# Layer 0 of a fused four-layer kernel: its setup and its units become one program, which also makes the start of layer 1

## Time and profile before

| what | value |
|---|---|
| median of 3 runs | 1658.1 us (1653.25 to 1659.24) |
| the profiled execution, its own time | 1658.67 us |
| its span, first to last instruction | 1656.9 us |
| mean granted TensorE clock | 0.971 |
| PE busy | 1541.7 us (93%) |
| DVE busy | 1102.9 us (67%) |
| ACT busy | 673.1 us (41%) |
| POOL busy | 451.4 us (27%) |

### The profile page before, as it was taken

The page is one execution under the profiler, slowest core; times in us unless marked ns, Lnnn a source line. Parts: engine busy times, 40 slices in busy tenths (PEclk is TensorE's granted clock), DMA queues, the critical chain, the costliest instruction groups (busy, mean ns, idle before and its releaser), DMA issues. The chain is left out here.

```text
span 1656.9 us, 33073 instructions
## 1 busy us (share of the span) xinstructions
PE 1541.7 (93%) x13299; PEld 1321.7 (80%) x13299; DVE 1102.9 (67%) x2371; ACT 673.1 (41%) x1270; POOL 451.4 (27%) x532
## 2 busy tenths in 40 slices
PE   4987999999999999999999999879988859999799
PEld 2666888888888888888888888869867747888598
DVE  6886666666666676666666667555599945676444
ACT  4654434343333434433343434432366633544322
POOL 2004120020101211210200200232188866653211
PEclk9998999999999999999999999889989979999899
DMA  4000010010000000000100100020030000000000
GB/s 132 1 0 26 14 39 14 1 39 14 27 14 14 27 14 14 27 14 14 39 14 1 39 27 1 30 45 1 2 115 2 1 1 2 2 2 3 1 26 25
DMA packets 44580, 34.16 MB, mean 21 GB/s; under 512 B 10770, under 2 KB 41496, under 8 KB 44312
## 3 DMA queue, kind: packets, MB, share of 16 engines
q1 hardware_dynamic: 44440, 32.17, 6.7%
HBM read 30.00 MB, written 2.10 MB: 19 GB/s over the span
## 5 line engine op out<-in xcount | busy, mean ns | idle before, releaser
L946 DVE STREAM_TRANSPOSE att_pt<-att_prob 32x256 f32<-32x256 f32 x496 | 215.9, 435 | 6.4
L846 ACT ACTIVATE g_q_sb<-psum,g_cols 128x512 f32<-128x512 f32 x128 | 88.4, 690 | 321.0 <-PE psum L714 321.0
L763 PE MATMUL psum<-g_wo_hi,att_ot_hi 128*128 128x256 f32 x512 | 150.2, 293 | 2.5 <-DVE att_ot_lo L959 1.4
L917 DVE TENSOR_REDUCE att_rmax<-psum 128x6 f32<-128x390 f32 (+1 forms) x96 | 49.2, 512 | 151.3 <-PE psum L676 151.3
L763 PE MATMUL psum<-g_wo_lo,att_ot_hi 128*128 128x256 f32 x512 | 145.5, 284 | 0.0
L763 PE MATMUL psum<-g_wo_hi,att_ot_lo 128*128 128x256 f32 x512 | 145.4, 284 | 0.0
L746 PE MATMUL psum<-att_pt,att_v_sb 128*128 128x128 f32 x1024 | 128.9, 280 | 3.5 <-DVE att_ot_lo L959 3.5
L969 DVE TENSOR_TENSOR g_x_res<-psum,g_x_res 128x256 f32<-128x256 f32 x128 | 54.3, 424 | 116.8 <-PE psum L763 88.5
L746 PEld LDWEIGHTS psum<-att_pt,att_v_sb 128*128 128x128 f32 x1024 | 123.2, 194 | 7.8 <-DVE att_ot_lo L959 3.7
L849 ACT ACTIVATE att_k_sb<-psum,g_cols 128x512 f32<-128x512 f32 x128 | 88.2, 689 | 81.0 <-PE psum L714 81.0
L714 PE MATMUL psum<-split_feat_hi,g_wide_hi 128*128 128x512 f32 x256 | 103.7, 405 | 4.5 <-DVE split_feat_lo L993 3.3
(11 more groups left out here) (301 smaller groups left out, 3936.5 us busy)
## 6 DMA issues: line engine op xcount, KB each, us to landing
g_ctx_f<-in_L_xattn_wq SPq DMA_DIRECT2D x32, 128.0 KB, 2.3
g_ctx_f<-in_L_xattn_wk SPq DMA_DIRECT2D x32, 128.0 KB, 2.8
g_ctx_f<-in_L_xattn_wv SPq DMA_DIRECT2D x8, 512.0 KB, 3.8
g_ctx_f<-in_L_xattn_wo SPq DMA_DIRECT2D x8, 512.0 KB, 3.8
c_ctx_tok<-in_ctx SPq DMA_DIRECT2D x4, 512.0 KB, 5.5
g_x_res<-in_x SPq DMA_DIRECT2D x4, 512.0 KB, 8.7
g_w<-in_L_xattn_mlp_w SPq DMA_DIRECT2D x2, 1024.0 KB
out<-g_x_res SPq DMA_DIRECT2D x8, 256.0 KB, 2.2
```

The source lines that it names most:

```text
L763: mm = pe.matmul(o_ps[p % 2], a, b, start=(h == 0 and t == 0), stop=(not last and h == HG - 1 and t == 2))
L846: act.activation(q_sb[:, h, :], q_ps[:, :], ACT.Identity, bias=G.cols[:, layer, head:head + 1]).then_inc(q_ready, 1)
L917: dve.tensor_reduce(rmax[:, a:b], s_ps[group][:, :, :], X_AXIS, ALU.max).then_inc(max_done, 1)
L946: turned = dve.transpose(pt[to:to + 32, :, :, r, u, 32 * a:32 * a + 32].rearrange("p h a t -> p (h a) t"), by_pair[of:of + 32, :, u, 32 * ...
```

## The change

`phase_setup` and `phase_layer0` become `phase_first`, one program, with its 18 steps (16 units, two of drain) written out and no loop. In it:

- The folding of `Wl` and `Wo` no longer waits for the constant rows; their transposes come on PE after unit 4, their copies on DVE after unit 5.
- ACT normalises 6 context tiles ahead of the units, and 5 each in units 0 and 1. DVE still normalises all 16 tiles of `x` ahead of unit 0, but each is announced by itself.
- POOL's copies of the context are gone: PE reads the context tile itself.
- SP issues layer 1's first weights right behind the constant rows.
- Work of layer 1's prologue moves in: DVE aggregates blocks 0 and 1 after units 8 and 11, POOL inverts; DVE normalises block 0 after units 10 and 12 (two tiles each); PE transposes it after units 13 and 14; ACT makes `raw` after the exponentials of 13 and 14, and the high parts after those of 14 and 15; DVE makes `feat_lo` in steps 16 and 17, behind the output of units 14 and 15; ACT and POOL split the weights of heads 0 and 1 in step 16.
- Layer 1's loop starts at j = 0. POOL's first work there, after a memset, is heads 2 and 3; DVE's is to normalise block 1, and then `wv_hi`, `wv_lo` and two memsets.

The core of the diff:

```diff
-                mm.then_inc(cols_psum, 1)
+                    if u == 4:
+                        pe.wait_ge(rows_in, n_rows)
+                        for i in range(2):
+                            mm = pe.transpose(cols_ps[:, i, :], rows[:, i, :], G.ident[0:ROWS, 0:ROWS])
+                        mm.then_inc(cols_psum, 1)
+                    if u in (13, 14):
+                        features(u - 13)
...
+                def features(k):
+                    pe.wait_ge(G.normed_done, PPB)
+                    pe.wait_ge(G.raw_done, k) if k else pe.wait_ge(cols_kept, 1)
+                    for i in range(PPB):
+                        mm = pe.transpose(x_bank[:, i * P:(i + 1) * P], w.normed[:, i, k * P:(k + 1) * P], G.ident[:, :])
+                    mm.then_inc(G.feat_psum, 1)
...
+                def normalize_context(p):
+                    act.activation(G.xn[:, PAIRS + p, :], G.ctx_tok[:, p, :], ACT.Identity,
+                                   bias=shift[:, p:p + 1], scale=rstd[0][:, p:p + 1]).then_inc(ctx_normed, 1)
+
+                def raw_features(k):
+                    act.wait_ge(G.feat_psum, k + 1)
+                    act.activation(w.raw[:, k, :], x_bank[:, :], ACT.Identity, bias=G.cols[:, 0, 82 + k:83 + k],
+                                   scale=G.cols[:, 0, 80 + k:81 + k]).then_inc(G.raw_done, 1)
+
+                def high_features(k):
+                    act.wait_ge(G.raw_done, k + 1)
+                    act.activation(G.feat_hi[:, k, 0:BLK], w.raw[:, k, :], ACT.Copy).then_inc(G.hi_done, 1)
...
+                    for p in range(EARLY + 5 * u, EARLY + 5 * u + 5):
+                        if p < PAIRS:
+                            normalize_context(p)
...
+                    if u in (13, 14):
+                        raw_features(u - 13)
+                    if u in (14, 15):
+                        high_features(u - 14)
+                    if u == PAIRS:
+                        act.wait_ge(arrived, 16 * len(w.first_loads))
+                        for h in range(2):
+                            act.activation(w.wqk_hi[:, h, :, :, :], w.stage_qk[:, h, :, :, :], ACT.Copy).then_inc(w_high, 1)
...
+                    if u in (8, 11):
+                        blk = (u - 8) // 3
+                        dve.wait_ge(G.stats_kept, PPB * (blk + 1))
+                        for p in range(PPB):
+                            dve.bn_aggr(G.mv[:, blk, p, :], G.stats[:, PPB * blk + p, :]).then_inc(G.mv_done, 1)
+                    if u in (10, 12):
+                        dve.wait_ge(G.rstd_done, 1)
+                        for p in (0, 1) if u == 10 else (2, 3):
+                            dve.tensor_scalar(w.normed[:, p, :], G.x_res[:, p, :], G.mv[:, 0, p, 0:1], G.rstd[:, 0, p:p + 1],
+                                              ALU.subtract, ALU.mult).then_inc(G.normed_done, 1)
+                    if u >= PAIRS:
+                        k = u - PAIRS
+                        dve.wait_ge(G.hi_done, k + 1)
+                        dve.tensor_tensor(G.feat_lo[:, k, 0:BLK], w.raw[:, k, :], G.feat_hi[:, k, 0:BLK].bitcast(F32),
+                                          ALU.subtract).then_inc(G.feat_ready, 1)
...
-                for j in range(-1, NI + 3):
+                for j in range(NI + 3):
```

More of the change, by code:

```diff
@@ L190, in _ @@
                         pool.tensor_tensor(rstd[t][:, ps], rstd[t][:, ps], G.minus_half[:, 0:PAIRS // 2], ALU.pow).then_inc(rstd_done[t], 1)
+                for blk in range(2):
+                    pool.wait_ge(G.mv_done, PPB * (blk + 1))
+                    r = G.rstd[:, blk, :]
+                    pool.tensor_scalar(r, G.mv[:, blk, :, 1], 1e-5, None, ALU.add).then_inc(G.eps_added, 1)
+                    pool.wait_ge(G.eps_added, blk + 1)
+                    pool.tensor_tensor(r, r, G.minus_half[:, 0:PPB], ALU.pow).then_inc(G.rstd_done, 1)
@@ new lines, in scores @@
+                def scores(u):
+                    pe.wait_ge(mix_done, u + 1)
+                    if u:
+                        pe.wait_ge(exp_done, 4 * u)
+                    for b in range(2):
+                        for th in range(2):
+                            mm = pe.matmul(s_ps[b][:, th, :], mix[64 * b:64 * b + 64, 0, th * P:th * P + P],
+                                           mix[64 * b:64 * b + 64, 1, :], start=True, stop=True)
+                        mm.then_inc(s_psum, 1)
@@ new lines, in outputs @@
+                def outputs(u):
+                    pe.wait_ge(t_act, u + 1)
+                    pe.wait_ge(t_dve, u + 1)
+                    if u:
+                        pe.wait_ge(x_done, u)
+                    for b in range(2):
+                        for sh in range(2):
+                            mm = pe.matmul(o_ps[64 * b:64 * b + 64, :], y_sb[u % 2][:, sh, 64 * b:64 * b + 64],
+                                           prob_t[:, b, sh, :], start=(sh == 0), stop=(sh == 1))
+                    mm.then_inc(o_psum, 1)
@@ new lines, in values @@
+                def values(u):
+                    if u:
+                        pe.wait_ge(y_done, u)
+                    for sh in range(2):
+                        mm = pe.matmul(y_ps[:, sh, :], G.ctx_tok[:, u, sh * P:sh * P + P], G.w_t[:, 2, :], start=True, stop=True)
+                    mm.then_inc(y_psum, 1)
+                def features(k):
[4 more added lines that the diff above has]
+                    mm.then_inc(G.feat_psum, 1)
@@ L214, in _ @@
                 pe.matmul(y_ps[:, 1, 0:1], G.w_t[:, 3, :], G.bias0[:, 2:3], start=True, stop=True).then_inc(g_psum, 1)
+                pe.wait_ge(lo_done, PAIRS)
+                for u in range(PAIRS + 2):
+                    if there(u):
+                        mix_in(u)
+                    if there(u - 2):
+                        turn(u - 2)
+                    if there(u):
+                        scores(u)
+                    if there(u - 2):
+                        outputs(u - 2)
+                    if there(u):
+                        if u == 0:
+                            pe.wait_ge(g_kept, 1)
+                        values(u)
+                    if u == 4:
+                        pe.wait_ge(rows_in, n_rows)
+                        for i in range(2):
+                            mm = pe.transpose(cols_ps[:, i, :], rows[:, i, :], G.ident[0:ROWS, 0:ROWS])
+                        mm.then_inc(cols_psum, 1)
+                    if u in (13, 14):
+                        features(u - 13)
```

334 lines of the change are left out of this document (126 added, 208 removed).

## The result

| what | before | after |
|---|---|---|
| median of 5 runs each, taken together | 1658.8 us (1653.25 to 1659.24) | 1642.77 us (1642.05 to 1645.03) |
| the profiled execution, its own time | 1658.67 us | 1642.77 us |
| its span | 1656.9 us | 1641.1 us |
| mean granted TensorE clock | 0.971 | 0.974 |

The account below looks back on a forecast made before the run. PE's idle time ahead of layer 1's first projection was taken to bound the kernel: start -6.5, units +4.3, drain +1.7, prologue -10.05, clock 0, sum -10.55 from 1658.67 gives 1648.1 us; range 1643.5 to 1653.

Parts of the forecast that it names:

- The prologue: Between layer 0's end on DVE and layer 1's first projection: 10.9 us shrink to 0.85, so -10.05 us.
- The start: Up to unit 0: folding no longer waits for the constant rows, PE mixes earlier; -6.5 us, bounds -8.0 and -6.0.
- I take all of it, since the only row of the kind shows a full stop: At the start: POOL's last power stops DVE's first normalisation for the full 1.5 us, out of nothing to 1.5.
- The tiles' cover of 0.4 us: Ahead of unit 0: the other 15 normalisations end at 32.5, 0.4 us before the first maxima are due at 32.9.
- Inserted work: Layer 0's units: 4.7 us of added work on DVE, PE and ACT, 0.4 off for the loop; +4.3 us.
- the tiles are hidden, with little to spare in unit 1: Units 0 and 1: ACT's five context tiles each, 2.5 us, fit where ACT waits and cost nothing.
- The drain: Behind layer 0's last units: two pieces of `feat_lo` on DVE at 0.88 us each, +1.7 us, bounds 0.9 and 2.2.
- The clock: Where layer 0 meets layer 1: same clock fall and cost as before, 0, bounds -2 (no fall) and +1.5 (lasts longer).
- a stretch behind the first projection that isn't as long as before: Sign of being wrong: everything behind layer 1's first projection was taken to move by the same amount, so 0 change there.
- more comes off: Rival, 0.20: two of no stop by the power (-1.5), clock kept (-2), insertions overlapping (-1.8); 1644.8 us.
- The slow one: Rival, 0.03: fetching layer 0's written-out steps stalls engines, perhaps 9 more packets at 2.8 us each, +25, 1673 us.
- The wait for heads 2 and 3: Layer 1's first step: PE might wait for POOL's weight split; forecast none, by a margin of 1 to 2 us.

Follow-up runs that it names:

- Experiment 1: The kernel after with layer 1's prologue put back into layer 1's loop, setup and layer 0 still one program: 1650.82 us, ratio 0.9965 to the kernel before.
- experiment 4: The kernel after with two unused POOL subtractions over 512 columns added behind its last power, beside DVE's normalisations of `x`: one run, 1645.57 us.
- experiment 3: The kernel before with layer 0's hardware loop written out and nothing else changed: 1658.16 us, ratio 1.0001.
- experiment 6: The kernel after with DVE's inserted work moved ahead of its wait for the exponentials, one tile each in units 9 to 12: 1642.1 us, ratio 0.991.
- Experiment 7: The kernel after with inserted work of DVE, PE, ACT and POOL moved into gaps: 1638.56 us, ratio 0.9891 to the kernel before.
- experiment 5: The kernel after with 38 unused transposes added on PE in idle places of layer 0's drain: 1641.26 us, ratio 0.9907 to the kernel before.
- experiment 2: The kernel after with its start undone: constant rows ahead of the folding, PE mixing only after all 16 tiles of `x`: 1649.82 us, ratio 0.9961.

## Why the prediction was right, and where it was off

The sign and the mechanism held: whatever brings the first projection forward shortens the whole. The range, 1643.5 to 1653, did not quite hold: 1642.77 lies 0.7 under it. The predicted time was 5.3 us too long. The steps follow; about 3.0 of the 5.3 are differences of the clock that no step forecast (-0.86 in the first units, +0.65 behind the first projection, -2.8 behind the first scores), so the total says less about the steps than the marks do.

- **The prologue**, -10.05: measured -10.04. Experiment 1 shows it from the other side, where 11.1 us stand there again.
- **The start**, -6.5: measured -7.94 to the first maxima. The step that failed is "I take all of it, since the only row of the kind shows a full stop". The row was of a POOL operation over 512 columns; experiment 4 reproduces that stop, and the power over 8 columns doesn't make one. The bound of -8.0 was the right value. The tiles' cover of 0.4 us held in the kernel after, and experiment 4 shows what lies behind it: with the tiles 2.0 later, the maxima were 1.6 later.
- **Inserted work**, +4.3: measured +3.29 from unit 0 to unit 15, made of -0.54 and +3.83. DVE took 2.23, not 2.7: 0.55 for the work on `cols` where 0.7 were put down, 0.46 for the aggregates where 0.7, 1.22 for the tiles where 1.3. PE and ACT took 1.61, not 2.0. The loop was worth nothing instead of 0.4 (experiment 3). The -0.54 was in no step. It is -0.86 from unit 0 to unit 1, because PE reached its full pace earlier (last section), and +0.32 from unit 1 to unit 2, for ACT's context tiles: "the tiles are hidden, with little to spare in unit 1" was the step that failed there. Without the -0.86 the term would be 4.15, close to the forecast because its errors cancel. Experiments 6 and 7 show that the cost came from the place in the queue, not from the work.
- **The drain**, +1.7: measured +1.01. The 0.88 a piece came from a row of `feat_lo`, from 133.25 to 135.02, beside which POOL was at work mostly on head 3's weights (timeline of the kernel before):

```profile
133.40 1.08 POOL L582 CAST g_wide_hi<-g_ctx_f 128x512 fp32r<-128x512 f32 x1
```

  Alone a piece takes 0.68, and since its record overlaps its neighbours', it adds 0.42 the first time and 0.58 the second. Experiment 7 has both durations: 1.12 beside POOL's low part, 0.68 the next time.
- **The clock**, 0: right for this drain in its order (the projections run at the low level for 5.2 us, before 4; 0.65 lost); that it moves at the next meeting too, for -2.1, was not seen. The bound of -2 stood for a clock that doesn't fall here, which only experiments 5 and 7 had.
- **What is left**, -0.7, lies behind layer 1's last outputs. That stretch is 578.0, 578.1 and 577.9 us in the kernel before and experiments 3 and 7, and 577.3 to 577.5 in all others: the same grouping as in layer 1's drain, so it may go with the clock too, which isn't shown; no single place was found for it. The prediction named a stretch behind the first projection that isn't as long as before as a sign of being wrong, and this sign came: 1519.6 against 1521.7.

Of the rivals, "more comes off" (1644.8) had the right first part, the power, and is nearer to the result than the forecast. But its other two parts, a clock that stays up and insertions that overlap, didn't happen, so the nearness is luck. The slow one is out by experiment 3. The wait for heads 2 and 3 never came; its margin was 3.6, not 1 to 2. What decides in which executions the clock falls inside the drain (experiments 1, 3, 4 and 6), behind it (the kernels before and after, experiment 2) or not at all (7) is open. The idle gap inside the drain is nearly the same in experiment 6 and the kernel after, 2.64 and 2.63, and in experiment 3 and the kernel before, 2.35 in both, with different outcomes.

## What to carry to other kernels

Put moved work in front of a wait of its engine, not behind it: the same tiles cost 0.61 a pair behind the copy and nothing ahead of the wait for the exponentials, where one tile (0.40) fits into the gap of each unit. Before a row is used as a price, look at what ran beside it, on POOL above all; both prices that were off here, the start's and the drain's, came from rows of DVE that a POOL operation over 512 columns had lengthened. And at drains compare from mark to mark: a place where the clock can fall moves the total by 1 to 2 us, as much as the edit that is being judged.

## What was unexpected in the hardware

- A POOL power over 8 columns leaves DVE's `tensor_scalar` alone (5.26 against 5.24 us for sixteen) and is itself slowed from 1.67 to 1.90; two POOL subtractions over 512 columns take 2.0 us from it.
- The granted clock reads 1.00 from the start of the span, but the first matmuls run at half the pace. In the kernel after the same four products take twice as long in units 0 and 1 as in unit 2 (timeline of PE):

```profile
26.37 2.04 PE L231 MATMUL psum<-split_xn,c_w_t 128*128 128x256 f32 x4 [0.94 <-issue]
32.36 1.92 PE L231 MATMUL psum<-split_xn,c_w_t 128*128 128x256 f32 x4
36.83 1.03 PE L231 MATMUL psum<-split_xn,c_w_t 128*128 128x256 f32 x4
```

  In the kernel before the third group, at 46.09, still took 1.43. So from unit 0 to unit 1 are 4.99 us instead of 5.85. Neither the early start nor the merging is needed for this: experiment 2 starts its units as late as the kernel before and has 4.68 us from unit 0 to unit 1, its scores there taking 1.14 where the kernel before needed 2.09, and experiment 3, the kernel before with its loop written out, has 4.67 with a first mixing at 34.25. What sets the moment is open.
- 38 transposes that nobody reads kept the clock up through a drain and were worth 2.0 us at the next mark.
